# A row table for gathers: GpSimd adds high and low halves on chip and each sum is stored once, in place of a store and an accumulating transfer

## The reference

```
x = x + gnn(layernorm(x)):
    h    = layernorm(x) @ W
    norm = 1/sqrt(deg[src]) * 1/sqrt(deg[dst])
    out  = segment_sum(h[src] * norm, dst) + b ; where(out > 0, out, prelu_a * out)
x = x + ffn(layernorm(x)):
    8 experts, 256 -> 512 -> 256 with gelu, the top 2 by a routing over the mean of all rows,
    weighted sum, + input, layer norm with gamma and beta
```

## Time and profile before

| | us |
|---|---|
| median of 3 runs | 1013.46 |
| lowest, highest | 1009.28, 1021.48 |
| the profiled execution | 1019.87 |
| its span, first to last instruction | 1017.9 |
| mean granted TensorE clock in it, as a share of 2.4 GHz | 0.989 |

### The profile page before, as it was taken

The page is one execution under the profiler, slowest core; times in us unless marked ns, Lnnn a source line. Parts: engine busy times, 40 slices in busy tenths (PEclk is TensorE's granted clock), DMA queues, the critical chain, the costliest instruction groups (busy, mean ns, idle before and its releaser), DMA issues.

```text
span 1017.9 us, 20363 instructions
## 1 busy us (share of the span) xinstructions
PE 991.0 (97%) x6991; PEld 839.4 (82%) x6992; DVE 844.9 (83%) x1720; ACT 514.9 (51%) x1006; POOL 532.6 (52%) x505
## 2 busy tenths in 40 slices
PE   8989989999999999999999999999899999999997
PEld 7767768888888888888888888888799999999996
DVE  6788868789988989989989889885777887878786
ACT  6486434444444444444444444443865647474641
POOL 4061288888888888888888888812001111111111
PEclk9799999999999999999999999999899999999999
DMA  9039956666666667657766666636211111111101
GB/s 306 14 106 270 180 135 153 160 159 155 159 155 157 167 146 170 160 124 171 163 148 163 160 155 159 149 68 234 74 33 53 41 46 46 46 46 46 45 22 36
DMA packets 70593, 126.76 MB, mean 125 GB/s; under 512 B 9876, under 2 KB 49934, under 8 KB 70510
## 3 DMA queue, kind: packets, MB, share of 16 engines
q0 software_dynamic: 33520, 90.35, 38.5%
q1 hardware_dynamic: 36990, 35.32, 10.9%
HBM read 66.93 MB, written 25.67 MB: 91 GB/s over the span
## 4 chain that ended last, share of the span: by engine, by line
PE 90%; DVE 4%; ACT 2%; issue 2%; DMA 1%; DVEq 0%; ACTq 0%; SPq 0%; POOLq 0%; another core or an unknown queue 0%
PE banks L1988 47%; PE banks L2097 13%; PE banks L1964 12%; PE banks L2111 8%; PE banks L2116 4%; PE banks L1829 3%; PE banks L1935 1%; DVE hot_src L1008 1%; PE banks L1819 1%; ACT gf L1759 0%; ACT gh L1757 0%; DVE hot_key L1008 0%; DMA dst_all<-in_dst 0%; ACT tab L1628 0%; DMA raw<-in_pairs,starts 0%
## 5 line engine op out<-in xcount | busy, mean ns | idle before, releaser
L1988 PE MATMUL banks<-tab,adj 128*128 128x512 f32 x2058 | 513.5, 399 | 1.3 <-ACT adj L1711 1.3
L1988 PEld LDWEIGHTS banks<-tab,adj 128*128 128x128 f32 x2058 | 375.1, 189 | 74.4 <-DVE tab L1121 1.5
L1706 ACT CAST adj<-banks 128x784 fp32r<-128x784 f32 x328 | 253.9, 815 | 334.6 <-PE banks L1964 314.9
L816 POOL DMA_INDIRECT fetched<-h_rows,node_row x252 | 318.4, 1263 | 76.5 <-issue 73.4
L1008 DVE TENSOR_TENSOR hot_src<-iota_src,turned 128x2048 bf16<-128x2048 bf16 x168 | 205.1, 1221 | 56.0 <-PE banks L1964 52.9
L1964 PEld LDWEIGHTS banks<-hot_key,hot_src 128*128 128x128 bf16 x2624 | 126.6, 98 | 47.2 <-issue 35.8
L1008 DVE TENSOR_TENSOR hot_key<-iota_key,turned 128x1568 bf16<-128x1568 bf16 x168 | 162.7, 969 | 0.0
L1964 PE MATMUL banks<-hot_key,hot_src 128*128 128x98 bf16 x2624 | 151.4, 209 | 4.5 <-issue 3.1
L2111 PE MATMUL banks<-W2s,gh 128*128 128x512 f32 x384 | 137.5, 399 | 0.5 <-DVE pre L1524 0.5
L1757 ACT ACTIVATE gh<-banks,b1e 128x384 fp32r<-128x384 f32 (+1 forms) x136 | 78.3, 575 | 88.7 <-PE banks L2097 88.5
L2116 PE MATMUL banks<-W2s,gl 128*128 128x256 f32 x392 | 110.0, 280 | 0.0
(11 more groups left out here) (257 smaller groups left out, 1103.5 us busy)
## 6 DMA issues: line engine op xcount, KB each, us to landing
partial<-fetched POOLq DMA_DIRECT2D x63, 512.0 KB
xin<-in_x SPq DMA_DIRECT2D x49, 128.0 KB
x_dram<-x SPq DMA_DIRECT2D x49, 128.0 KB
x1f<-x_dram POOLq DMA_DIRECT2D x16, 384.0 KB, 3.7
out<-res SPq DMA_DIRECT2D x48, 128.0 KB, 1.7
h_rows<-tab SPq DMA_DIRECT2D x5, 1024.0 KB, 15.0
h_rows<-tab POOLq DMA_DIRECT2D x5, 1024.0 KB, 15.1
W1a<-in_W POOLq DMA_DIRECT2D x8, 512.0 KB, 6.2
```

The lines of the kernel that those rows point to most:

```text
L816: g.indirect_dma_start(out=into, out_offset=None, in_=h_rows, in_offset=bass.IndirectOffsetOnAxis(ap=node_row[:, k, r - 1:r], axis=0), bou ...
L1706: s.copy(adj[k][:, :].rearrange("p (q n) -> p q n", n=P)[:, :, at:at + 2 * BANK_NODES].rearrange("p q (b n) -> p q b n", b=2), bank_pairs[ ...
L1988: last = mm(acc[k][:, :], adj[k][:, q * P:(q + 1) * P], tab[:, q, :], start=(at == 0), stop=(at == T - 1), skip_group_check=True)
```

## The change

`h_rows` is now made by GpSimd itself. In 13 parts (12 of 4 blocks, taken in turn from the direct and the held half, and the last block alone) it waits for DVE's low halves of the part, adds high and low from `tab` in SBUF into one of the buffers `fetched[:, 1]` and `fetched[:, 2]` in turn, and SP stores the buffer as soon as it is written. A buffer is written again only after its store has landed. SP's stores of high halves, the six accumulating transfers and their semaphores are gone. The tenants of the early region may no longer reach into the two buffers.

```
-    TABLE_PARTS = ((0, 8), (HELD, 32), (8, 16), (32, 40), (16, HELD), (40, T))
+    TABLE_PARTS = [(at + 4 * j, at + 4 * j + 4) for j in range(HELD // 4) for at in (HELD, 0)] + [(T - 1, T)]
...
-        room = tenants(ROOM_AT, ADJ_AT)
+        room = tenants(ROOM_AT, ROOM_AT + 3 * WIDE * D * WORD)
         W = room("W", [P, KD, D + 1])
...
+        def row_sums(i):
+
+            lo, hi = TABLE_PARTS[i]
+            return fetched[:, 1 + i % 2, 0:hi - lo, :]
+
+        def rows_stored(eng):
+
+            for k in range(2):
+                eng.wait_ge(row_sums_stored[k], len(TABLE_PARTS[k::2]) * 16)
...
                 for i, (lo, hi) in enumerate(TABLE_PARTS):
-                    if lo < HELD:
-                        sp.wait_ge(hi_fixed, hi)
-                    else:
-                        sp.wait_ge(hi_made, hi - HELD)
-                    sp.dma_start(h_rows[lo * P:hi * P, :].rearrange("(t p) d -> p t d", p=P), tab[:, lo:hi, 0:D].bitcast(F32)).then_inc(hi_stored[i // 2], 16)
-                sp.wait_ge(h_summed, 16 * len(TABLE_PARTS))
+                    sp.wait_ge(row_sums_made, i + 1)
+                    sp.dma_start(h_rows[lo * P:hi * P, :].rearrange("(t p) d -> p t d", p=P), row_sums(i)).then_inc(row_sums_stored[i % 2], 16)
+                rows_stored(sp)
...
-                def add_low_rows(i):
+                def make_row_sums(i):
 
                     lo, hi = TABLE_PARTS[i]
                     if lo < HELD:
                         pool.wait_ge(lo_fixed, hi)
                     else:
                         pool.wait_ge(lo_made, hi - HELD)
-                    pool.wait_ge(hi_stored[i // 2], 32)
-                    g.dma_start(h_rows[lo * P:hi * P, :].rearrange("(t p) d -> p t d", p=P), tab[:, lo:hi, D:2 * D].bitcast(F32),
-                                accum_op=ALU.add).then_inc(h_summed, 16)
+                    if i >= 2:
+                        pool.wait_ge(row_sums_stored[i % 2], i // 2 * 16)
+                    g.tensor_tensor(row_sums(i), tab[:, lo:hi, 0:D].bitcast(F32), tab[:, lo:hi, D:2 * D].bitcast(F32), ALU.add).then_inc(row_sums_made, 1)
...
                 for i in range(len(TABLE_PARTS)):
-                    add_low_rows(i)
-                pool.wait_ge(h_summed, 16 * len(TABLE_PARTS))
+                    make_row_sums(i)
+                rows_stored(pool)
```

More of the change, by code:

```diff
@@ L134, in gnn_ffn_kernel @@
     N_STARTS = N_KEYS + len(LISTED)
-    TABLE_PARTS = ((0, 8), (HELD, 32), (8, 16), (32, 40), (16, HELD), (40, T))
+    TABLE_PARTS = [(at + 4 * j, at + 4 * j + 4) for j in range(HELD // 4) for at in (HELD, 0)] + [(T - 1, T)]
+    assert T - 1 == 2 * HELD and HELD % 4 == 0 and WIDE == 4 and FETCHED == 3
     LAST = (ND - 1) % 2
@@ L424, in gnn_ffn_kernel @@
         lo_made = sem("lo_made")
-        hi_stored = [sem(f"hi_stored{i}") for i in range(len(TABLE_PARTS) // 2)]
-        h_summed = sem("h_summed")
+        row_sums_made = sem("row_sums_made")
+        row_sums_stored = [sem(f"row_sums_stored{k}") for k in range(2)]
         node_src_in = [sem(f"node_src_in{k}") for k in range(2)]
```

## The result

The changed kernel takes 1032.82 us (median of 4 runs, 1032.02 to 1035.13). The kernel before, run beside it, takes 1013.61 us (1009.28 to 1021.48). The ratio is 1.0184, with a 95% interval of 1.0119 to 1.0249. A second set of runs of the same kernel gave 1032.69 us and 1.0201 [1.0161, 1.0241]. So the change makes the kernel 19.2 us slower.

The account below looks back on a forecast made before the run. PE, busy 97% of the span, was taken as the bound, so only its lateness counts. Removal 0 plus 13 us of DVE lateness at the first count took 1013.5 to 1026.5 us, range 1010 to 1038.

Parts of the forecast that it names:

- The removal at 0: Removing six stores of about 1 MB and six accumulating transfers, hidden under PE, was costed at 0.
- The hold in both directions: GpSimd instructions reading SBUF and DVE instructions with two SBUF inputs run one after the other, each engine waiting; +13 us.
- The one weak row of 0.1 us: Trace sign for DVE waiting on GpSimd: L965 takes 1.94 us where L973, as wide, takes 1.84 us.
- the first count: In the sizing: exclusive use by DVE and GpSimd in the table stage, less its 27.1 us, gives 11.0 us too much.
- second count: Table stage: each sum holds DVE for 1.8 us; 10.5 sums, less 3.4 us of DVE idle time, give 15.5 us.
- less the 3.4 us that DVE idles: DVE's idle time in the 27.1 us of the table stage, subtracted from the hold of the sums.
- I count nothing for them: Sums after the table stage meet windows where DVE has a tenth of its time left; costed at nothing.
- 16 us of margin: DVE adds up a gathered block's parts some 16 us after GpSimd issues the last addition; gathers are off the chain.
- the starved case: Second rival: GpSimd seldom gets in, sums slip into windows, rows complete at 150 to 170 us; about 1038 us, chance 0.08.
- The hole: Around 130 to 146 us in the profile before, a window 4.9 us too long, taken as something other runs lack.
- the third rival: Lighter traffic removes up to 4.9 us of hole: 1008.6 us without a hold (chance 0.07), 1021.6 with it.
- No hold: First rival: only GpSimd waits and DVE streams on, so sums cost nothing, 1013.5 us; no or small hold, chance 0.27.

Follow-up runs that it names:

- Without sums: Changed kernel, but SP stores the high halves part by part and GpSimd adds nothing, so rows lack their low halves: 1012.77 us, 0.9973.
- the sums alone: Kernel before with its stores and accumulating transfers kept, plus GpSimd's thirteen sums, whose results are not used: 1040.25 us, ratio 1.0244.
- the memsets: Changed kernel with a memset of the same tile in place of each GpSimd addition, so gathered rows are zero: 1011.91 us, 0.9961.
- the late sums: Changed kernel with GpSimd's sums started only after DVE's one-hot tiles of the second block, so they fall into the first windows: 1035.98 us, 1.0190.
- the small sums: Changed kernel with 49 sums of one block (128x256) in place of 13, stores as they are: 1019.93 us, 1.0040.
- the kernel with PE kept busy: Changed kernel plus unused 128x128 matmuls on PE in the places where it waited for DVE: 1030.71 us, 1.0150.

## Why the prediction was right, and what it mis-sized

The direction and the mechanism were right: +13 us forecast (range 1010 to 1038), +19.2 measured.

*The removal at 0.* Held. Without sums the time is 0.9973 of that before, with an interval that holds 1. The rows completed earlier and nothing came of it.

*What a sum takes.* 2.2 us was close: 2.3 us unheld (4.67 / 2). The Trainium skill's "GPSIMD Engine Reference", section "Performance versus the Vector engine", had led to an estimate of 2.25 us, and the trace agrees.

*The hold in both directions.* Confirmed by the sums alone (+24.9 us) against the memsets (none). The one weak row of 0.1 us in the trace before pointed the right way, but that is partly luck: it compares two operations with different inputs (int32 and float32 against two of float32), and it reads 1.94 against 1.84 or 1.85 us in the later profiles too, so it may never have shown a hold. The Trainium skill's "SBUF — State Buffer", section "Who interferes with whom", has the two engines share a read interface as an exclusive lock, and says of DVE's two-port modes that the first to issue keeps it for its whole instruction. Most holds here fit one GpSimd instruction. But a DVE operation was also held through two (5.54 us) and through four (5.41 us, and 10.79 us in the kernel of the sums alone), longer than the rule's words let one expect.

*The size, where the sum failed.* The step is "10 or 11 of them lie in it: ... 11.0 by the first count, and ... 15.5 by the second ... I take the middle". Its second count, 12 x 1.8 + 0.2 = 21.8 us of holding, was right: 20.7 us of lengthening. Three of its deductions were not.
- All thirteen sums lay in the stage (67.1 to 110.4 us), not 10 or 11. A store landed in 2.9 us and not in 4, and the first sum started 2.8 us earlier with its stage. This is worth 21.8 - 10.5 x 1.8 = 2.9 us.
- "less the 3.4 us that DVE idles" was not got back: over the whole stage DVE idled 5.5 us before L1121 in the kernel before and idles 6.3 us before L1129 now, 5.5 of them for ACT. PE and ACT had stopped behind DVE and had to start again, which is argued from the order of the rows and was not tried apart. Worth 3.4 us.
- The first count, "exclusive use" of 42.0 us in 27.1, let DVE's other 8.6 us (23.6 - 15.0) run beside the sums. But DVE works in order, and behind a held operation its PSUM work waits as well. Averaging with that bound took 15.5 - 13.2 = 2.3 us off.

These three bring 13.2 back to 21.8 us; the stage was 20.9 us longer. The median rose by less, 19.2, and the 2.6 us that the kernel without sums gained may be the rest.

*"I count nothing for them" (the sums in the windows).* Wrong as a rule, without effect here since no sum fell there. In the late sums 24.2 us of holds cost the windows 17.8 us, and the late gathers behind them 6.9 more: with the rows complete at 138 us the "16 us of margin" is used up. In the small sums 9.0 us of short holds cost them 3.3 us.

*The lower clock.* The prediction had it only under the starved case. It came without starvation, at 0.51 from 72 to 84 us, from PE's waits for DVE. By the kernel with PE kept busy it is part of the undersizing, 1 to 5 us, most of it within the 20.9 us of the stage.

*The hole.* "I take it for something that other runs lack" is neither shown nor refuted. Eight profiles lack it, but none of their kernels has the accumulating transfers. The one other kernel with them, that of the sums alone, lacks it too, with its gathers starting straight behind the transfers. This speaks against the third rival's mechanism, that the lighter traffic removes the hole, but it is one profile, and its sums had moved its windows. If the hole were in every run of the kernel before, the kernel without sums should gain 5.4 us; it gained 2.6, between -1.1 and 6.5 us by its interval. That decides nothing, and a second profile of the kernel before would. What is settled is that this part is small beside the hold.

*The rivals.* No hold: excluded by DVE's lengthened rows. Starved sums: excluded by the gathers' start at 116.32 us.

## What to carry to other kernels

An idle GpSimd is not free room: count each of its two-input SBUF operations at its full length against DVE's two-input work, and ask whether DVE has that time before PE wants its tiles. Where such work must go there, try it in small pieces and measure each size (one block each cost 3.7 us, two blocks each 18.7, four blocks each 19.2), or give it a form with one input where the work allows (1.1 us against the kernel before, 3.7 against the one without sums), and compare with DVE doing it itself (11.9 us). None of the versions tried that makes the whole sum beats the store with an accumulating transfer, whose traffic was hidden. And where such work is put off instead, look at what GpSimd has to do behind it: the late sums lost 6.9 us to gathers that came too late, 440 us further on.

## What was not expected of the hardware

- Some DVE operations were held through several GpSimd instructions in a row: 5.54 us through two of 128x1024, 5.41 us through four of 128x512, 10.79 us through four of 128x1024 (the sums alone). Most were held through one. With instructions of 128x256 the longest excess was 0.6 us.
- A DVE operation with a single SBUF tile, L1254 over 128x39 float32, was held as well: 1.62 us against 0.24. L1263 over 128x128 float32 was held even beside a memset: 1.07 us against 0.28. An operation with one tile in SBUF and one in PSUM (L1129, 25 times) never was, 485 ns at most.
- A GpSimd copy of 128x1024 takes 1.04 us undisturbed and held seven DVE operations by 5.3 us in all, over thirteen copies; a memset of 0.96 us held none with two SBUF inputs.
